# A fused layer with a routed feed-forward part: the tile map in four parts, one rank step and one square root moved

## The reference

```python
n = layernorm(x)
h[t] = diag(A) * h[t-1] + B @ n[t]
x = x + C @ h + D * n

n = layernorm(x)
shared = (silu(n @ shared_gate.T) * (n @ shared_up.T)) @ shared_down.T
logits = n @ gate_w.T
e = argmax(logits); score = sigmoid(max(logits))
routed = the same feed-forward part with expert e's weights, on n * score
x = x + shared + routed
```

## Time and profile before

| | us |
|---|---|
| runs shown: median (lowest, highest) | 280.53 (279.43, 281.22) |
| the profiled execution, its own time | 280.06 |
| its span | 277.8 |
| TensorE busy | 235.3 |
| VectorE busy | 177.2 |
| ScalarE busy | 172.3 |
| GpSimd busy | 146.1 |

### The profile page before, as it was taken

How to read it: one execution, slowest core, us unless ns; L and a number is a source line. 1 busy time by engine, 2 the same in 40 slices (tenths; PEclk the granted TensorE clock), 3 DMA queues, 4 the chain that set the end, 5 groups by cost and what they waited for, 6 DMA issues and landing times. The chain is left out here.

```text
span 277.8 us, 6120 instructions
## 1 busy us (share of the span) xinstructions
PE 235.3 (85%) x1891; PEld 181.2 (65%) x1891; DVE 177.2 (64%) x512; ACT 172.3 (62%) x415; POOL 146.1 (53%) x150
## 2 busy tenths in 40 slices
PE   0595979979779999999599899999999999999900
PEld 0254466566457456767276799999999999765700
DVE  3799998799887976659952256655555565534200
ACT  2844898887897965633134889776777684523400
POOL 1000000027777757778781036777777777775950
PEclk9999597979999999999889999999999999999975
DMA  7999500002323222323944924454555443211992
GB/s 207 383 355 327 211 0 2 1 19 100 116 99 115 105 78 99 119 97 119 318 150 139 296 94 120 136 165 128 176 170 168 132 119 107 77 49 48 106 172 26
DMA packets 24862, 37.83 MB, mean 136 GB/s; under 512 B 3680, under 2 KB 16864, under 8 KB 24272
## 3 DMA queue, kind: packets, MB, share of 16 engines
q1 hardware_dynamic: 15264, 22.03, 25.9%
q0 software_dynamic: 9568, 15.41, 19.9%
HBM read 22.03 MB, written 19.73 MB: 150 GB/s over the span
## 5 line engine op out<-in xcount | busy, mean ns | idle before, releaser
L1045 POOL DMA_INDIRECT table<-rows,place x64 | 65.8, 1027 | 61.9 <-DVE place L815 43.0
L1086 POOL DMA_INDIRECT out<-w_full x51 | 49.3, 967 | 32.9 <-DVE w_full L1015 18.6
L441 PE MATMUL bank<-xT_hi,w_split 128*128 128x256 f16 (+1 forms) x156 | 41.1, 264 | 0.5 <-DVE xT_lo L1000 0.5
L443 PE MATMUL bank<-xT_hi,w_split 128*128 128x256 f16 (+1 forms) x156 | 41.1, 264 | 0.0
L442 PE MATMUL bank<-xT_lo,w_split 128*128 128x256 f16 (+1 forms) x156 | 40.9, 263 | 0.0
L593 ACT ACTIVATE n1T<-bank,g_scale 128x512 f32<-128x512 f32 x32 | 21.8, 687 | 28.8 <-PE bank L395 22.7
L453 PE MATMUL bank<-w_full,hid 128*128 x284 | 38.6, 277 | 0.2
L453 PEld LDWEIGHTS bank<-w_full,hid 128*128 128x128 f32 x284 | 34.8, 192 | 1.5 <-issue 0.4
L871 DVE SCALAR_TENSOR_TENSOR hid<-bank,h_scale,n1T 128x512 f32<-128x512 f32 x32 | 23.3, 747 | 15.3 <-ACT n1T L593 14.3
L407 PEld LDWEIGHTS bank<-w_full,hid 128*128 128x128 f32 x256 | 31.4, 195 | 2.1 <-issue 0.3
L407 PE MATMUL bank<-w_full,hid 128*128 128x128 f32 x256 | 31.5, 277 | 0.0
(11 more groups left out here) (142 smaller groups left out, 439.5 us busy)
## 6 DMA issues: line engine op xcount, KB each, us to landing
w_full<-table SPq DMA_DIRECT2D x24, 264.0 KB, 4.0
rows<-in_x SPq DMA_DIRECT2D x8, 512.0 KB, 7.6
w_full<-in_weights SPq DMA_DIRECT2D x3, 1152.0 KB, 12.0
table<-in_pads SPq DMA_DIRECT2D x1, 2112.0 KB, 9.2
table<-in_pads SPq DMA_DIRECT2D x8, 264.0 KB, 4.5
x_ring<-table SPq DMA_DIRECT2D x8, 264.0 KB, 3.8
out<-rows POOLq DMA_DIRECT2D x8, 256.0 KB, 7.9
table<-rows,place POOLq DMA_INDIRECT x64, 2.4
```

Of the source, the lines that this page charges most:

```text
L441: mm(o, w_of(kind, e, 0, c), xT_hi[k][:, 0:w], start=True, stop=False)
L443: last = mm(o, w_of(kind, e, 1, c), xT_hi[k][:, 0:w], start=False, stop=True)
L1045: g.indirect_dma_start(table[:, :], bass.IndirectOffsetOnAxis(ap=place[:, i:i + 1], axis=0), rows[:, i, :], None).then_inc(done, 16)
L1086: g.indirect_dma_start(out[:, :], bass.IndirectOffsetOnAxis(ap=x_in[k][:, s, 2 * D:2 * D + 1].bitcast(I32), axis=0), x_in[k][:, s, 0:D], N ...
```

## The change

1. On TensorE `ranks(2)` moves from block 2, ahead of `shared_down(1)`, to block 1, behind `shared_down(0)`. On VectorE `places(2)` moves from ahead of `base(1)` in b == 2 to behind `base(0)` in b == 1.
2. On ScalarE `std1(1)`, the root for the second pair, moves from ahead of both copies of the first pair to behind them.
3. `tile_map()`, called at b == 7 on VectorE, becomes four functions with the same instructions in the same order, called at b == 7, 9, 10 and 11. Each instruction keeps its increment and wait.

```diff
@@ TensorE, loop over the shared blocks
-                if b == 2:
-                    ranks(GROUPS - 2)
                 if b == 4:
                     logits(GROUPS - 1)
                 if b == 5:
                     ranks(GROUPS - 1)
                 if b >= 1:
                     shared_down(b - 1)
+                if b == 1:
+                    ranks(GROUPS - 2)
@@ ScalarE, first stage
-                if s + 2 < PAIRS:
+                if s + 2 < PAIRS and s != -1:
                     std1(s + 2)
                 if -1 <= s < LAST:
                     copy_n1T(s + 1, 0)
...
                 if -1 <= s < LAST:
                     copy_n1T(s + 1, 1)
+                if s == -1:
+                    std1(1)
@@ VectorE
-            def tile_map():
-                steps = [0]
...
+            def map_counts():
                 dve.wait_ge(s_count, 1)
...
+                map_ready(v.tensor_tensor_scan(end_whole[:, 1:E + 1], ones_e, whole_f[:], 0.0, ALU.mult, ALU.add))
+
+            def map_singles():
+                map_ready(v.tensor_scalar(end_whole[:, 1:E + 1], end_whole[:, 1:E + 1], float(WHOLE), None, ALU.min))
...
+                map_ready(v.tensor_tensor(out=single_gain[:], in0=next_gain[:], in1=single[:], op=ALU.subtract))
...
+            def map_experts():
...
+            def map_rows():
                 v.tensor_scalar(tile_expert_f[:], tile_expert_f[:], 1.0, float(E), ALU.add, ALU.min)
...
+                map_ready(v.tensor_scalar(tile_weights[:], tile_expert_f[:], float(F), None, ALU.mult))
+                assert map_steps[0] == MAP
@@ VectorE, loop over the shared blocks
-                if b == 2:
-                    places(GROUPS - 2)
                 if 1 <= b <= EARLY:
                     base(b - 1)
+                if b == 1:
+                    places(GROUPS - 2)
...
                 if b in (6, 8):
                     routed_weights_lo((b - 6) // 2)
                 if b == 7:
-                    tile_map()
+                    map_counts()
+                if b == 9:
+                    map_singles()
+                if b == 10:
+                    map_experts()
+                if b == 11:
+                    map_rows()
```

More of the change, by code:

```diff
@@ L919, in _, with map_ready, map_spread @@
                     route(s // GROUP - 1)
-            def tile_map():
-                steps = [0]
[L923 to L932, removed]
+            map_steps = [0]
+            def map_ready(instruction):
+                instruction.then_inc(s_map, 1)
+                map_steps[0] += 1
+                dve.wait_ge(s_map, map_steps[0])
+            def map_spread(values, n):
+                return values[:, None, :].to_broadcast([P, n, E])
+            def map_counts():
                 dve.wait_ge(s_count, 1)
-                ready(v.tensor_copy(pad_place[:], count_bank))
-                ready(v.tensor_tensor(out=count_f[:], in0=count_bank, in1=region_of, op=ALU.subtract))
+                map_ready(v.tensor_copy(pad_place[:], count_bank))
+                map_ready(v.tensor_tensor(out=count_f[:], in0=count_bank, in1=region_of, op=ALU.subtract))
                 v.memset(end_whole[:, 0:1], 0.0)
@@ L943, in tile_map @@
                 v.tensor_copy(halves_f[:], halves_i[:])
[L944 to L947, removed]
-                ready(v.scalar_tensor_tensor(out=single[:], in0=whole[:, 0:E], scalar=-2.0, in1=halves_f[:],
-                                             op0=ALU.mult, op1=ALU.add))
@@ L950, in tile_map @@
-                ready(v.tensor_scalar(single[:], single[:], 0.0, None, ALU.max))
+                map_ready(v.tensor_copy(whole_f[:], whole_i[:]))
+                map_ready(v.tensor_tensor_scan(end_whole[:, 1:E + 1], ones_e, whole_f[:], 0.0, ALU.mult, ALU.add))
+            def map_singles():
+                map_ready(v.tensor_scalar(end_whole[:, 1:E + 1], end_whole[:, 1:E + 1], float(WHOLE), None, ALU.min))
+                map_ready(v.tensor_tensor(out=whole[:, 0:E], in0=end_whole[:, 1:E + 1], in1=end_whole[:, 0:E],
+                                          op=ALU.subtract))
+                map_ready(v.scalar_tensor_tensor(out=single[:], in0=whole[:, 0:E], scalar=-2.0, in1=halves_f[:],
+                                                 op0=ALU.mult, op1=ALU.add))
+                map_ready(v.tensor_scalar(single[:], single[:], 0.0, None, ALU.max))
@@ L959, in tile_map @@
                     number = const[:, col["tile_no"]][:, 0:n]
-                    ready(v.tensor_tensor(out=ended[:, tiles, :], in0=spread(end, n),
-                                          in1=number[:, :, None].to_broadcast([P, n, E]), op=ALU.is_le))
-                ready(v.tensor_reduce(tile_expert_f[:], ended[:], AX, ALU.add))
+                    map_ready(v.tensor_tensor(out=ended[:, tiles, :], in0=map_spread(end, n),
+                                              in1=number[:, :, None].to_broadcast([P, n, E]), op=ALU.is_le))
@@ L963, in tile_map @@
+                map_ready(v.tensor_reduce(tile_expert_f[:], ended[:], AX, ALU.add))
                 for tiles, end, gain in (by_whole, by_single):
                     n = tiles.stop - tiles.start
-                    ready(v.tensor_tensor(out=ended[:, tiles, :], in0=ended[:, tiles, :], in1=spread(gain, n), op=ALU.mult))
+                    map_ready(v.tensor_tensor(out=ended[:, tiles, :], in0=ended[:, tiles, :], in1=map_spread(gain, n),
+                                              op=ALU.mult))
```

27 lines of the change are left out of this document (13 added, 14 removed).

## The result

| | before | after |
|---|---|---|
| median of 22 runs each, us (lowest, highest) | 280.47 (279.19, 281.91) | 281.29 (280.14, 282.33) |
| ratio after / before, 95% interval | | 1.0032 (1.0018 to 1.0045) |
| the profiled execution, us | 280.06 | 280.18 |
| its span | 277.8 | 277.9 |
| closing additions begin | 256.89 | 257.34 |

The forecast was 280.7 and "within 1%". The profiled execution of the changed kernel, 280.18, is the third fastest of its 22 and only 0.12 above that of the kernel before. So the traces side by side account for 0.1 us and not for the whole 0.8 of the medians.

What follows compares the result with a forecast made beforehand. GpSimd's row stores were taken to set the end, with TensorE's blocks nearly level. Ranks -1.83, root +1.08, stores' delays -0.4 and clock +1.35 summed to +0.2 us: 280.7 on the median, no change, range 279.9 to 281.5.

Steps and rivals of the forecast that it cites:

- Ranks, -1.83: Third group's ranks and places one block sooner: GpSimd's stores to the table come 1.83 us sooner.
- Root, +1.08: Second pair's root behind the copies: VectorE's first scan moves from 14.62 to 15.70, a loss of 1.08 us nothing absorbs.
- rival 2: First stage takes the root's delay back, so its move costs nothing: -0.9 us, 279.6; chance 0.17.
- Stores' delays, -0.4: GpSimd stores held beside VectorE's two weight splits: shifted issues gain 0.4 us, between a 1.6 gain and a 1.0 loss.
- First load 148.1: SyncE's first tile load follows the last store by 2.99 us, at 148.1, just behind the map's condition at 147.9.
- From load to transposition: Time from the first tile load's issue to TensorE's first transposition: 6.52 us, as before, so transposition at 154.6.
- TensorE ready at 150.7: With its hole and slow stretch gone, TensorE would be ready for the first tile at 150.7.
- Idle 3.9, clock +1.35: TensorE idles 3.9 us before the first transposition; its clock drops, making the last shared products 1.35 us longer.
- Rival 1: TensorE's clock stays up at the seam before the first tile: -1.15 us, 279.4; chance 0.15.
- Rival 3: TensorE's clock returns late: 282.4, or 283.8 with bad store delays; chance 0.08 over 1% slower, 0.10 milder.
- The sum, +0.2: Ranks, root, stores' delays and clock together: +0.2 us, 280.3 for the profiled execution, 280.7 on the median, no change.
- Rival 4: TensorE's 5.1 us from the removed hole and slow stretch comes through: 275.4, or 277.5 for what remains possible; chance 0.09.

Runs made afterwards that it cites:

- g4: Changed kernel with the second pair's root back in place and 30 unread products before the first tile's transposition on TensorE; 278.55 us, 0.9951 of the kernel before.
- f1: Changed kernel with SyncE's wait for the whole map put behind its waits for the row stores; 281.58 us, 1.0040 of the kernel before.
- g1: Changed kernel with the second pair's root back ahead of the copies, first kind of chip; 280.07 us, 0.9985 of the kernel before.
- f2: Changed kernel with 30 unread 128x256 products on TensorE ahead of the first tile's transposition; 279.55 us, 0.9967 of the kernel before.
- e2: Kernel before with the root's move alone, second kind of chip; 326.89 us, 1.0008 of the kernel before.
- g2: Kernel before with the map in parts alone, first kind of chip; 281.25 us, 1.0042 of the kernel before.
- e1: Changed kernel with the second pair's root back ahead of the copies, second kind of chip; 327.37 us, 1.0045 of the kernel before.
- e3: Kernel before with the map in parts alone, second kind of chip; 330.65 us, 1.0133 of the kernel before.
- g6: Changed kernel with 24 small unread products behind the map's closing counts on TensorE, second kind of chip; 330.41 us, 1.0049 of the kernel before.
- g5: g4 with 24 small unread products behind the map's closing counts on TensorE, second kind of chip; 329.80 us, 1.0026 of the kernel before.
- e4: Kernel before with the third group's ranks and places one block sooner, alone, second kind of chip; 320.52 us, 0.9849 of the kernel before.

## Why the prediction was right, step by step

- **Ranks, -1.83.** Right for the stores: 1.86 in g4, where the root does not interfere; places ready at 101.68 in after.
- **Root, +1.08.** Right at the first scan. It began at 15.42, not 15.70, because all of after's first pair came 0.27 sooner (its input landed at 4.27, before at 4.54); from there it is 1.07. That "nothing absorbs it" is not borne out: in f1 only 0.20 was left at the first places. The prices in the times are 1.3 give or take 0.8 (after against g1), 0.4 give or take 1.1 (f2 against g4) and 0.3 give or take 0.9 (e2). So rival 2 (no cost) fails in after's trace and is in part what f1's shows; the times don't settle the size.
- **Stores' delays, -0.4.** The three longer stores are 3.14 over the norm, before 3.46: -0.32. The store at 134.95 ended 0.85 behind the end of the split of 133.86, as in both cases of before (0.85 and 0.84). The Trainium skill (SBUF — State Buffer, on the two separate sides) would also have a two-input comparison hold a store; the trace agrees: the store at 141.18 took 1.10 beside the comparison at 141.02 and ended 0.84 behind its end, which costs 0.13.
- **Last store 145.1.** It was 145.13. So close a match is partly luck: f1, the same but for SyncE's waits, has it at 144.42.
- **First load 148.1.** This step failed: "2.99 us after GpSimd issued the last store" was carried over, and it became 4.36. Of the lengthening, 1.37, the last closing packet has 1.20 (3.26 against 2.06), and it came late behind the instruction packet. The map was done at 147.07 (forecast 147.3), and SyncE did not wait for it.
- **From load to transposition.** It failed too, the other way: taken as 6.52 and measured 5.24 (154.73 minus 149.49). ScalarE began 3.84 us behind the load instead of 5.11. The two errors are +1.39 and -1.28, and the traces make them one: the instruction packet has moved from the load to the stores. ScalarE's first step needs the first two tiles. Of the sixteen parts in which the second one's load lands, fifteen were there 3.80 us behind the first load in before and the last at 5.02; in after all sixteen by 3.75. Last store to tanh is 8.10 before and 8.20 after. That two wrong steps cancelled, so that the transposition came at 154.73 for a forecast 154.6, was luck.
- **TensorE ready at 150.7.** It was 150.71, but the forecast's terms don't give that: 5.1 sooner less 0.88 is 4.22 sooner, thus 151.05, an idle time of 3.55 and a margin of the load against the map of nothing instead of 0.2. The trace has 4.56.
- **Idle 3.9, clock +1.35.** Idle 4.02, the products 1.23 longer, the lower level from 155.5 to 158.9. Rival 1 is out; f2 shows what it would have given: 0.9967, or -0.9, beside the -1.15 of the forecast. Rival 3 is out: routed products follow every 0.11 us from 158.91.
- **First routed product 158.9.** It was 158.91, 0.19 behind before; the sum had +0.2. The third result came 0.34 later and the end 0.45; the 0.26 between is not accounted for.
- **The sum, +0.2.** The traces side by side have +0.1, the medians +0.8, and their interval (0.5 to 1.3) leaves the sum out: "no change" was right, and so was the mechanism at the seam, but the sum was short by some 0.6. Where that lies is open. Two things differ enough from one execution to the next: the first stage (f1 and after, 0.7 apart at the first places) and the landing of the last store (first load 4.36 behind it in after's profile, 4.78 and 4.93 in f1's and f2's).
- **The hole's 5.1 us goes into a new wait.** Right, and the sharper form is g2's: alone, the map in parts is a loss of 1.2 us. Rival 4 is out: SyncE did wait for the stores, and on the second kind of chip for the map.

The large change in the trace, a hole and a slow stretch of TensorE removed, moved the end by next to nothing because TensorE was not the last at the seam; and by itself (g2) it lost 1.2 us, since the time came back there as an idle stretch with a slow clock behind it, on the path, and a longer landing of the last store.

## What to carry to other kernels

Before a stall is removed, look at where the engine will wait instead, and what its clock does there: a slow stretch that was hidden can come back on the path. Where the engine had to wait at such a seam, thirty products that nobody reads kept the clock up, and were worth about as much as the best of the three edits. Take the edits one by one, too: one gained a microsecond, one lost as much, the third lost up to as much, and together they looked like no change. And where two steps of a forecast are wrong by as much in opposite directions, its end says nothing of them.

## What the runs showed of the hardware

**The clock after a wait.** TensorE's idle time before the first transposition and the sixteen products behind it, by kernel: 0.66 and 1.95 (g4), 1.47 and 1.95 (f2), 2.00 and 1.95 (e1), 2.05 and 1.95 (e3), 2.15 and 1.95 (g6); 4.02 and 3.18 (after), 4.44 and 3.36 (f1), 4.85 and 3.62 (g1), 5.50 and 3.62 (g2). The Trainium skill (TensorE: Matmul & The Clock Gate, HAM oscillation) describes waits for data that throttle the array; the trace agrees, with these sizes.

**Instruction packets among the data.** Each profile has 17 packets of q8 (g5 has 18), 0.28 MB in all or some 16 KB each. The one that stands nearest to the last store took from 0.92 to 1.60 us, where the store's own data packets took under 0.5, and the landings differ as in the table above.

**The first stage's clock.** It differs between executions whose first stage is the same code: from 45 to 50 us it was 0.87 in after and 1.00 in f1. With it the time from the fourth to the fifth scan goes from 11.9 to 12.7 us (see g1 above).

**Two kinds of chips.** On the second kind the same kernel takes 16% longer. TensorE's timeline shows pauses in which it waits for nothing that the profile knows, between the logits' products that follow one another every 0.025 us otherwise (e2):

```profile
69.67 0.17 PE L357 MATMUL bank<-router_split,n2T_hi 128*128 128x8 f16 x1
70.80 0.17 PE L358 MATMUL bank<-router_split,n2T_lo 128*128 128x8 f16 x1 [0.96 <-issue]
71.53 0.17 PE L356 MATMUL bank<-router_split,n2T_hi 128*128 128x8 f16 x1 [0.56 <-issue]
72.23 0.19 PE L357 MATMUL bank<-router_split,n2T_hi 128*128 128x8 f16 x1 [0.54 <-issue]
73.65 0.17 PE L358 MATMUL bank<-router_split,n2T_lo 128*128 128x8 f16 x1 [1.23 <-issue]
```

Instructions that arrive late would look so; no run tested it. There the first load waits for the map wherever the map is in parts (e1, e3, g5, g6), and the parts have other prices: the ranks gain 1.5% instead of 0.35%, the map in parts loses 1.3% instead of 0.4%. Why the ranks gain so much there stays open. Of the 6.3 us between the first routed products of e2 and e4 (184.00 and 177.66) 4.4 are there at the third group's places (116.81 and 112.44), more than the 1.83 of the ranks and the 1.08 of the root.
